# Gated cross-attention block on one core: a fifth key chunk of two row tiles goes the way of the squares, V's last two tiles change banks, row facts keep their layout

## What is computed

```python
def attention(x, ctx, wq, wk, wv, wo):          # x is layer-normed: (4, 512, 512)
    q = einsum('bsd,ed->bse', x, wq)
    k = concatenate([ctx, einsum('bsd,ed->bse', x, wk)], axis=1)   # 512 old + 512 new keys
    v = concatenate([ctx, einsum('bsd,ed->bse', x, wv)], axis=1)
    attn = softmax(einsum('bqd,bkd->bqk', q, k) / sqrt(512))
    return einsum('bqd,ed->bqe', einsum('bqk,bkd->bqd', attn, v), wo)
def ffn(x, up, down, up_scale, down_scale, output_scale):         # 512 -> 2048 -> 512
    hidden = relu(einsum('bsd,hd->bsh', x, sign(up)) * up_scale)
    return einsum('bsh,dh->bsd', hidden, sign(down)) * down_scale * output_scale
x = x + tanh(g_xattn) * attention(layernorm(x), ...)
x = x + tanh(g_ffn) * ffn(layernorm(x), ...)
```

## Time and profile before

| | |
|---|---|
| median of 3 runs | 578.27 us (578.03 to 578.69) |
| the profiled execution | 578.35 us |
| its span | 576.6 us, 6972 instructions |
| granted TensorE clock, mean | 0.999 of full speed |
| PE busy | 572.0 us (99%), 2642 matmuls |
| DVE busy | 397.9 us (69%) |
| ACT busy | 280.8 us (49%) |
| POOL (GpSimd) busy | 123.0 us (21%) |
| DMA | 59.97 MB in 93392 packets, 71856 of them under 512 B |

### The profile page before, as it was taken

One profiled execution on the slowest core, in us unless ns is written; L12 is line 12 of the kernel. 1 busy time (PEld: TensorE's weight loads), 2 busy tenths in 40 slices (PEclk: granted clock), 3 DMA queues, 4 the chain that ended last, 5 costly groups with the idle time before them and its releaser, 6 DMA issues.

```text
span 576.6 us, 6972 instructions
## 1 busy us (share of the span) xinstructions
PE 572.0 (99%) x2642; PEld 476.4 (83%) x2642; DVE 397.9 (69%) x560; ACT 280.8 (49%) x401; POOL 123.0 (21%) x109
## 2 busy tenths in 40 slices
PE   9999999999999999999999999999999999999997
PEld 7988888888888888888888888888888888888886
DVE  5889546688685588682588686777569545766655
ACT  4784512564321564321565454756468355555531
POOL 5006222102033002033012043332322022422000
PEclk9999999999999999999999999999999999999999
DMA  8612752124414145425114833373811311330011
GB/s 313 229 62 37 184 181 75 44 67 114 106 74 73 41 179 151 105 76 73 66 44 108 257 110 109 95 161 112 211 43 36 147 37 38 108 112 36 5 70 73
DMA packets 93392, 59.97 MB, mean 104 GB/s; under 512 B 71856, under 2 KB 76208, under 8 KB 92976
## 3 DMA queue, kind: packets, MB, share of 16 engines
q1 hardware_dynamic: 93360, 59.54, 35.6%
HBM read 44.84 MB, written 14.69 MB: 103 GB/s over the span
## 4 chain that ended last, share of the span: by engine, by line
PE 98%; DVE 1%; DMA 0%; issue 0%
PE proj L674 28%; PE score L790 19%; PE turn L775 13%; PE score L708 9%; PE score L674 8%; PE turn L674 8%; PE proj L775 5%; PE proj L708 4%; PE score L923 2%; PE turn L666 1%; PE score L666 1%; PE turn L998 0%; DMA rows<-in_x 0%; PE score L998 0%; PE score L915 0%; DVE stats L1631 0%
## 5 line engine op out<-in xcount | busy, mean ns | idle before, releaser
L790 PE MATMUL score<-down_signs,hid_split 128*128 128x512 f32 x480 | 128.4, 390 | 0.0
L790 PEld LDWEIGHTS score<-down_signs,hid_split 128*128 128x128 f32 x480 | 89.2, 188 | 18.4 <-DVE hid_split L1690 0.5
L674 PE MATMUL proj<-four_x,weights 128*128 128x512 f32 x336 | 76.8, 389 | 0.0
L674 PEld LDWEIGHTS proj<-four_x,weights 128*128 128x128 f32 x336 | 63.0, 188 | 13.0
L606 POOL TENSOR_TENSOR four_x<-raw_ctx,four_x 128x2048 fp32r<-128x2048 f32 x7 | 32.6, 4654 | 132.4 <-ACT four_x L1029 132.4
L1690 DVE TENSOR_TENSOR hid_split<-hid,hid_split 128x512 fp32r<-128x512 f32 x64 | 44.4, 696 | 16.0 <-ACT hid_split L1245 15.8
L775 PE MATMUL turn<-ops_b,up_ops 128*128 128x512 f32 x192 | 51.3, 389 | 0.0
L1245 ACT ACTIVATE hid_split<-hid 128x512 fp32r<-128x512 f32 x64 | 40.0, 630 | 21.4 <-PE turn L998 13.7
L1236 ACT ACTIVATE hid<-hid,hid_gain 128x512 f32<-128x512 f32 x48 | 34.8, 724 | 22.7 <-DVE hid L1719 11.1
L674 PE MATMUL score<-weights,four_x 128*128 128x512 f32 x192 | 45.3, 389 | 0.0
L674 PE MATMUL proj<-weights,four_x 128*128 128x512 f32 x192 | 45.3, 391 | 0.0
(11 more groups left out here) (146 smaller groups left out, 947.5 us busy)
## 6 DMA issues: line engine op xcount, KB each, us to landing
raw_w<-in_ffn_w SPq DMA_DIRECT2D x21, 512.0 KB, 3.4
raw_ctx<-in_ctx_turned SPq DMA_DIRECT2D x4, 1024.0 KB, 5.2
raw_ctx<-in_ctx SPq DMA_DIRECT2D x4, 1024.0 KB, 5.4
probs_rows<-probs_squares SPq DMA_DIRECT2D x64, 64.0 KB, 1.9
squares_placed<-probs_rows SPq DMA_DIRECT2D x8, 512.0 KB, 4.5
raw_x<-block_rows SPq DMA_DIRECT2D x4, 1024.0 KB, 7.2
result<-rows SPq DMA_DIRECT2D x15, 256.0 KB, 2.0
rows<-in_x SPq DMA_DIRECT2D x3, 1024.0 KB, 9.7
```

Of the source, the lines that this page charges most:

```text
L674: last = pe.matmul(bank, lhs(l), rhs(r), start=start and i == 0, stop=stop and i == 2)
L790: last = pe.matmul(wide(r), hid_split[:, n % HR, s, r * P:(r + 1) * P], down_signs[:, chunk_of(q), :], start=(q == 0 and s == HI), stop=(q ...
```

## The change

Row tiles 2 and 3 now send five chunks of 128 keys through the squares (`FAR`), the four old ones and the first new one, and PE turns only three for them. `probs_squares` is [128, 4, 640] and lies over `qT`. SP stores three tiles, places half 0, stores the fourth tile and places half 1. v2 and v3 go to the banks `score[0]`, and the turns stand inside v2, after its first two products. The new terms take key chunks 1, 2 and 3 first and chunk 0 last, behind the wait for half 0. The row facts are stored as they lie in SBUF, so that `all_facts` is [128, 128, 2, 4], and the norming reads a fact at a step of 8 elements (32 bytes).

```diff
--- before.py
+++ after.py
@@ -101,7 +101,7 @@
         turned_x = at("turned_x", 208, [P, DC, ROWS])
         raw_w = at("raw_w", 216, [P, 1024])
         raw_late = at("raw_late", 204, [P, 1024])
-        all_facts = at("all_facts", 216, [P, 2, ROWS])
+        all_facts = at("all_facts", 216, [P, P, 2, RT])
 
 
         raw_q = at("raw_q", 120, [P, DC, ROWS])
@@ -160,17 +160,19 @@
         late_squares = normed
 
 
+        FAR = {2: RT + 1, 3: RT + 1, 0: RT, 1: RT}
+        FAR_ALL = RT + 1
         PAIRS = ((2, 3), (0, 1))
-        probs_squares = at("probs_squares", 160, [P, RT, ROWS])
+        probs_squares = at("probs_squares", 112, [P, RT, FAR_ALL * P])
         squares_placed = at("squares_placed", 176, [P, KC, ROWS])
-        probs_rows = nc.dram_tensor("probs_rows", (BATCH, ROWS, ROWS), F32).ap()
+        probs_rows = nc.dram_tensor("probs_rows", (BATCH, FAR_ALL * P, ROWS), F32).ap()
         probs_rows_v = probs_rows.rearrange("b (c p) q -> b p c q", p=P)
         probs_squares_v = probs_rows.rearrange("b (j n) (t i a) -> b t i n j a", n=SQ, i=P // SQ, a=SQ)
 
         def placed_part(h):
 
             first = PAIRS[h][0] * P
-            return slice(None), slice(0, RT), slice(first, first + 2 * P)
+            return slice(None), slice(0, FAR[PAIRS[h][0]]), slice(first, first + 2 * P)
 
         def scaled(c, r):
 
@@ -200,7 +202,7 @@
 
         squares_v = block_rows.rearrange("b (j a) (r i n) -> b i a r j n", a=SQ, i=P // SQ, n=SQ)
         rows_away = nc.dram_tensor("rows_away", (P, 2 * RT, DIM), F32).ap()
-        row_facts = nc.dram_tensor("row_facts", (BATCH - 1, 2, RT, P), F32).ap()
+        row_facts = nc.dram_tensor("row_facts", (BATCH - 1, P, 2, RT), F32).ap()
         block_stats = sb("block_stats", [P, RT, 6])
         block_mean_var = sb("block_mean_var", [P, RT, 2])
         block_var_eps = sb("block_var_eps", [P, RT])
@@ -231,11 +233,17 @@
 
             return turn[:, n % 4, :] if n % 4 < 2 else score[1][:, n % 4 - 2, :]
 
+        def turned_cols(n):
+            return 4 * P if n < RT else KEYS - FAR[TILE_ORDER[n % RT]] * P
+
         def proj_bank(n):
             if n < DC:
                 return wide(n)
 
+
             i = (n - PROJS_FIRST) % PROJS_BATCH
+            if n >= PROJS_FIRST and i in (2, 3):
+                return score[0][:, i - 2, :]
             return turn[:, i - 6, :] if n >= PROJS_FIRST and i in (6, 7) else proj[:, n % 2, :]
 
         small_in, ctx_in, out_stored = map(sem, ("small_in", "ctx_in", "out_stored"))
@@ -452,18 +460,27 @@
 
             def place_squares(b):
 
-                for h, pair in enumerate(PAIRS):
-                    for t in pair:
-                        sp.wait_ge(probs_squared, tile_done(b, t))
-                        for i in range(P // SQ):
-                            sp.dma_start(probs_squares_v[b, t, i], probs_squares[i * SQ:(i + 1) * SQ, t].rearrange(
-                                "n (j a) -> n j a", a=SQ)).then_inc(squares_stored[h], 16)
+                def store_tile(t):
+                    sp.wait_ge(probs_squared, tile_done(b, t))
+                    far = FAR[t] * P // SQ
+                    for i in range(P // SQ):
+                        sp.dma_start(probs_squares_v[b, t, i][:, 0:far],
+                                     probs_squares[i * SQ:(i + 1) * SQ, t, 0:far * SQ].rearrange("n (j a) -> n j a", a=SQ)
+                                     ).then_inc(squares_stored[t not in PAIRS[0]], 16)
+
+                def place(h):
+                    sp.wait_ge(squares_stored[h], 2 * STORED * (b + 1))
+                    first, last = PAIRS[h]
+                    sp.dma_start(squares_placed[placed_part(h)],
+                                 probs_rows_v[b][:, 0:FAR[first], first * P:(last + 1) * P]).then_inc(placed[h], 16)
+
+                for t in TILE_ORDER[:3]:
+                    store_tile(t)
 
                 sp.wait_ge(scored, product_scored(b, A22, 1))
-                for h, pair in enumerate(PAIRS):
-                    sp.wait_ge(squares_stored[h], 2 * STORED * (b + 1))
-                    cols = slice(pair[0] * P, (pair[1] + 1) * P)
-                    sp.dma_start(squares_placed[placed_part(h)], probs_rows_v[b][:, :, cols]).then_inc(placed[h], 16)
+                place(0)
+                store_tile(TILE_ORDER[3])
+                place(1)
 
             def block_rows_back(b):
                 sp.wait_ge(squares_out[b], STORED)
@@ -484,13 +501,12 @@
 
                 sp.wait_ge(rstd_done, b)
                 sp.wait_ge(means_out, b)
-                sp.dma_start(row_facts[b - 1].rearrange("s r p -> p s r"), mean_rstd[:, :, :],
-                             allow_slow_non_contiguous=True).then_inc(facts_stored, 16)
+                sp.dma_start(row_facts[b - 1], mean_rstd[:, :, :]).then_inc(facts_stored, 16)
                 sp.wait_ge(facts_stored, 16 * b)
 
                 sp.wait_ge(scored, product_scored(b - 1, S3, 1))
-                sp.dma_start(all_facts[:, :, :], row_facts[b - 1:b].rearrange("a s r p -> a s (r p)").broadcast_to(
-                    [P, 2, ROWS])).then_inc(facts_in, 16)
+                sp.dma_start(all_facts.rearrange("i p s r -> i (p s r)"), row_facts[b - 1:b].rearrange(
+                    "a p s r -> a (p s r)").broadcast_to([P, 2 * ROWS])).then_inc(facts_in, 16)
 
             for b in range(BATCH):
                 context_rows(b)
@@ -667,7 +683,7 @@
                 last.then_inc(turned, 1)
 
             def cols(src):
-                return [src[:, k * P:(k + 1) * P] for k in range(4)]
+                return [src[:, k * P:(k + 1) * P] for k in range(src.shape[1] // P)]
 
             def product(bank, lhs, rhs, start, stop):
                 for i, (l, r) in enumerate(PASSES):
@@ -748,7 +764,7 @@
             def turn_probs(b, i):
                 t = TILE_ORDER[i]
                 pe.wait_ge(exp_done, tile_done(b, t))
-                turn_job(turn0(b) + i, cols(probs[:, t, ROWS:KEYS]))
+                turn_job(turn0(b) + i, cols(probs[:, t, FAR[t] * P:KEYS]))
 
             def v_jobs(b):
 
@@ -757,15 +773,14 @@
                 for r in range(RT):
                     if r < 2:
                         pe.wait_ge(score_c11, 2 * b + r + 1)
-                    else:
-                        pe.wait_ge(proj_lo, values_out(b, r - 2))
+                    elif r == 2:
+                        pe.wait_ge(score_sums, 10 * (b + 1))
                     for i, (lhs, rhs) in enumerate(v_terms(r)):
                         last = product(proj_bank(proj0(b) + r), lhs, rhs, i == 0, i == DC - 1)
+                        if r == 2 and i == 1:
+                            for k in range(RT):
+                                turn_probs(b, k)
                     last.then_inc(proj_done, 1)
-                    if r == 1:
-                        pe.wait_ge(score_sums, 10 * (b + 1))
-                        for i in range(RT):
-                            turn_probs(b, i)
 
             def up_product(g, k, bank, left, i, start, stop):
 
@@ -855,14 +870,21 @@
                 n = proj0(b)
                 pe.wait_ge(turn_lo, turn0(b) + RT)
 
+
+
+                pe.wait_ge(proj_lo, values_out(b, 2))
+                for e in (0, 2):
+                    for i in (1, 2):
+                        product(proj_bank(n + DC + e), *new_terms(e)[i], i == 1, False)
+                pe.wait_ge(proj_lo, values_out(b, 3))
+                for e in (0, 2):
+                    last = product(proj_bank(n + DC + e), *new_terms(e)[3], False, False)
+                for e in (1, 3):
+                    for i in (1, 2, 3):
+                        last = product(proj_bank(n + DC + e), *new_terms(e)[i], i == 1, False)
+                pe.wait_ge(placed_lo, 2 * b + 1)
                 for e in range(DC):
-                    if e == 1:
-                        pe.wait_ge(proj_lo, values_out(b, 3))
-                    for i, (lhs, rhs) in enumerate(new_terms(e)):
-                        if e == 0:
-
-                            pe.wait_ge(proj_lo, values_out(b, max(i, 2)))
-                        last = product(proj_bank(n + DC + e), lhs, rhs, i == 0, False)
+                    last = product(proj_bank(n + DC + e), *new_terms(e)[0], False, False)
                 if last_batch:
                     last.then_inc(new_read, 1)
                 pe.wait_ge(placed_lo, 2 * b + 2)
@@ -1030,7 +1052,7 @@
 
             def turn_out(n, dst):
                 act.wait_ge(turned, n + 1)
-                act.activation(dst, four(turn_bank(n)), ACT.Copy).then_inc(turn_hi, 1)
+                act.activation(dst, four(turn_bank(n)[:, 0:turned_cols(n)]), ACT.Copy).then_inc(turn_hi, 1)
 
             def proj_out(n, dst):
                 act.wait_ge(proj_done, n + 1)
@@ -1112,14 +1134,11 @@
 
             def probs_out(b, i):
                 t = TILE_ORDER[i]
-                turn_out(turn0(b) + i, probsT[:, HI, RT:KC, t * P:(t + 1) * P])
```

(24 more changed lines are left out.)

## The result

The changed kernel takes 588.72 us (median of 5 runs, 586.8 to 588.97) beside 578.38 for the kernel before (5 runs): a ratio of 1.0173, 95% interval 1.0158 to 1.0187. It is slower by 10.3 us, where 577.4 was forecast and the range ended at 580.8. The profiled execution has a span of 586.8 us, 10.2 more than before.

The account below looks back on a forecast made before the run. PE, busy 99% with no wait to remove, was taken to bound the kernel. -0.87 us for the transposes and 0 for the three other terms gave 577.48 from 578.35, median 577.4; range 577.0 to 580.8.

Parts of the forecast that it names:

- PE's saving: PE's turns of row tiles 2 and 3: 8 transposes fewer at 0.109 us each in the chain, 0.87 us gained.
- rival 2: PE's transposes: each is worth its full duration, 8 x 0.273 = 2.18 us, giving 576.1 us; chance 0.05.
- V's banks, the turns inside V and the new order of the new terms: PE's V and new terms in each batch: the changed waits and order were to cost nothing.
- I take 2.29, the row of the same engine and shape: DVE's two norming instructions: strided facts leave each at 2.29 us, no more than before, so no cost.
- The upper bound of 4.65: DVE's norming instruction: at most 4.65 us, what the same subtraction takes GpSimd.
- The bounds of half 1: Half 1's low part, ahead of the old terms: between 0.7 us earlier and 1.3 later, at least 3.2 slack, no cost.
- Rival 3: Placed squares: half 0 or 1 comes late through queueing behind 640 KB or a stalled issue; 578 to 580 us; chance 0.09.
- The cover: 36 and 48 matmuls of new terms on PE hide the loads of half 0 and half 1, so they cost nothing.
- rival 1: Strided norming on DVE delays Wo's chunk 2: 4.5 us an instruction, 2.7 to 5.3 us in sum, about 581; chance 0.20.
- The facts' store: Store of the row facts in 32-byte runs: lands in 2 to 4 us for 13.0, nothing waits, gain nothing.

Follow-up runs that it names:

- e4: Changed kernel with contiguous row facts as before and all four row tiles stored ahead of both loads back: 577.45 us, ratio 0.9977.
- e3: Kernel before with only the change's row facts added (layout, store, load, strided norming): 579.51 us, ratio 1.0014.
- e5: Changed kernel with ten extra unused matmuls between Wo's chunk 1 and chunk 2 pieces in batches 1 and 2: 584.44 us, ratio 1.0103.
- e1: Changed kernel with the row facts stored, loaded and read contiguously as before: 577.50 us, ratio 0.9979.
- e8: Changed kernel with all stores ahead of both loads back and the pair squares behind chunk 3, strided facts kept: 577.56 us, ratio 0.9986.
- e7: Kernel before with twelve unused DVE instructions over 512 elements at its end, operands at various steps: 586.29 us in one execution.
- e2: Changed kernel with all four row tiles stored ahead of both loads back, strided facts kept: 583.95 us, ratio 1.0080.

## Why the prediction was wrong

- **PE's saving** held: 8 transposes, 14 of them in 1.53 us a batch in e4's chain, and 1.0 us measured for 0.87. The price by distance in the chain was the right one; the 2.18 us of rival 2 were not seen. V's banks, the turns inside V and the new order of the new terms cost nothing.
- **The failed step is "I take 2.29, the row of the same engine and shape".** The norming instructions take 4.05 and 4.17 us. The row had the same shape but not the same access, and the edit was about the access. The upper bound of 4.65 was nearer, and the rule on 16-byte lines that the prediction cites from the Trainium skill named the pattern; that rival had a chance of 0.20. Taken alone this step was worth 1.0 us (e3), which the range would have held; it takes the next two to make 10.3.
- **The bounds of half 1 failed too**: "between 0.7 earlier and 1.3 later" was 3.9 later. Moving the fourth tile's stores behind a 640 KB load doubled their landing (4.4 us for about 2), and half 1's load waits for just that landing. Rival 3 named the queueing and gave it no number. Half 0's load, too, was issued at 147.24, only 0.9 us earlier than before and not 2.4: the 12 stores ahead of it took 8.87 us, 0.74 each for the 0.60 counted. The cover held, but not as computed: the old terms never waited for half 1, though in batch 1 its low part ended at 159.58 and their row starts at 160.10, 0.5 us for the "at least 3.2" forecast. What failed was the view that cover on PE is all there is: a late half 1 also pushes DVE's whole queue behind it.
- **The sum of the parts.** The forecast set each delay against the slack of one consumer, and only rival 1 added two of them. Rival 1's place and mechanism are what happened. Its price, 2.7 to 5.3 us, was short by two terms: half 1's real delay instead of at most 1.3, and the slow clock, 3.1 us in the two batches, for which there was no term at all. Batch 0, for which it gave 0.5, had no stall.
- **The facts' store** landed after 5.6 us instead of 13.0, not 2 to 4, and nothing waited for it, as forecast.

What is left open: which property of the two gaps decides whether the clock falls. e5 shows only that it stays when the longer gap is filled.

## What to carry to other kernels

Delays of different edits that end in the same in-order queue use up one slack: add them before comparing, since here parts worth +1.0 and -1.0 us alone made +10.3 together. Look at what stands between the delayed instruction and the read-out that the bound engine waits for; moving that filler gave 9.0 us back, where undoing the facts gave 11.2 and undoing the split of the stores 4.8. Price an edit of an access pattern by the pattern, and keep a small store that someone waits for ahead of a large load. e1, e4 and e8 are each faster than both kernels; e4, at 577.45, is the fastest by a difference that these runs do not resolve.

## What the runs showed of the hardware

- DVE in fp32: an operand with a step of 16 to 64 bytes raises `tensor_tensor` over 512 elements from 0.69 us to between 1.01 and 1.07 (e7), and one of 32 bytes over 2048 from 2.3 to 4.1; 8 bytes is free, 12 cost 0.14 us. At 32 bytes it makes no difference which operand is strided, or whether both are.
- PE's granted clock fell to 0.50 behind gaps of 1.55 and 2.59 us, and in batch 2 behind gaps of 0.89 and 2.59, each pair 2.72 us of work apart, and stayed there for some 3 us of full work. In e2's profiled execution single gaps of 2.37 and 2.60 us left it at 1.00; four of e2's six runs have a mean clock of 0.997 and are longer. One of 29 runs of the kernel before has 0.993 and took 583.07 us, and no trace shows where it fell.
- A 64 KB store of 32x32 squares landed in a median of 1.9 us where both loads were issued behind all stores (before, e2, e4), and in 3.9 to 4.9 where it was issued behind a 640 KB load of the same queue (tile 1's four stores in each batch of the changed kernel).
